# A conditioned mixture-of-experts layer on one core: the first batch's h in plain f32, casts in another place, and the last rows weighed by VectorE and TensorE

## The reference

```python
h = einsum('bsi,bio->bso', x, W[id]) + b[id][:, None, :]      # (4, 256, 256), 16 experts of W, one for each batch
y = swiglu(h, sw1, sw2, sw3)                                   # shared: silu(h @ sw1) * (h @ sw3) @ sw2, width 352
scores = softmax(h @ gate_w)                                   # 8 experts, each row takes its two highest
for e in range(8):
    y = y + cw[:, e:e + 1] * swiglu(h, rw1[e], rw2[e], rw3[e]) # width 176; cw is 0 where e was not chosen
out = x + y
```

## Time and profile before

| | us |
|---|---|
| median of 3 runs (lowest, highest) | 115.42 (114.95, 117.1) |
| the profiled execution: its own time | 114.82 |
| the profiled execution: its span | 113.2 |

### The profile page before, as it was taken

How to read it: one execution, slowest core, us unless ns; L and a number is a source line. 1 busy time by engine, 2 the same in 40 slices (tenths; PEclk the granted TensorE clock), 3 DMA queues, 4 the chain that set the end, 5 groups by cost and what they waited for, 6 DMA issues and landing times.

```text
span 113.2 us, 2194 instructions
## 1 busy us (share of the span) xinstructions
PE 104.1 (92%) x608; PEld 88.2 (78%) x608; DVE 68.0 (60%) x220; ACT 52.2 (46%) x131; POOL 47.7 (42%) x63
## 2 busy tenths in 40 slices
PE   6997998499999978999999999999999999999870
PEld 4776887466688856677889998999999997888650
DVE  1034864546999079878877775684754533123991
ACT  4044673762660295366655753456556545102200
POOL 5280078872777200005653345335535536703610
PEclk9999999959999999999999999999999999999999
DMA  2897999996988446431232424231021120029935
GB/s 36 247 309 240 349 362 360 372 393 174 228 254 274 185 142 188 125 110 60 93 133 73 143 84 136 88 128 54 5 93 40 52 92 0 0 23 381 376 122 210
DMA packets 16736, 19.07 MB, mean 168 GB/s; under 512 B 2338, under 2 KB 13718, under 8 KB 16726
## 3 DMA queue, kind: packets, MB, share of 16 engines
q1 hardware_dynamic: 13302, 12.62, 36.3%
q0 software_dynamic: 1984, 4.46, 11.2%
q10 hardware_dynamic: 1440, 1.86, 4.9%
HBM read 12.64 MB, written 7.21 MB: 175 GB/s over the span
## 4 chain that ended last, share of the span: by engine, by line
PE 60%; ACT 8%; DVE 7%; another core or an unknown queue 7%; issue 6%; DMA 5%; POOL 3%; POOLq 1%; DVEq 0%; ACTq 0%
PE bank L858 42%; PE bank L870 6%; DVE x_area L815 5%; PE bank L1027 4%; PE bank L992 4%; ACT w_all L494 4%; DMA y_area<-_out_by_choice_and_token 3%; ACT cond_area L462 2%; DMA _out_by_choice_and_token<-y_area,dest 2%; ACT hT_area L443 1%; PE bank L885 1%; PE bank L888 1%; POOL _out_by_choice_and_token L412 1%; POOLq L289 1%
## 5 line engine op out<-in xcount | busy, mean ns | idle before, releaser
L412 POOL DMA_INDIRECT _out_by_choice_and_token<-y_area,dest x23 | 23.6, 1025 | 38.0 <-DVE y_area L771 26.3
L858 PE MATMUL bank<-w_all,hsT_hi 128*128 x72 | 21.6, 342 | 0.0
L396 POOL DMA_INDIRECT rows_by_expert<-h_area,slot x16 | 15.7, 978 | 12.8 <-DVE slot L634 8.7
L858 PE MATMUL bank<-hT_area,sh_area 128*128 128x512 f32 (+1 forms) x72 | 18.6, 418 | 0.0
L858 PEld LDWEIGHTS bank<-hT_area,sh_area 128*128 128x128 f32 (+1 forms) x72 | 13.4, 190 | 4.1 <-DVE sh_area L552 0.3
L858 PEld LDWEIGHTS bank<-w_all,hsT_hi 128*128 128x128 f32 x72 | 13.0, 188 | 0.0
L765 DVE TENSOR_TENSOR y_area<-y_area,bank 128x176 f32<-128x176 f32 x23 | 7.7, 336 | 7.3 <-issue 4.2
L509 ACT ACTIVATE y_area<-bank 128x176 f32<-128x176 f32 x23 | 7.3, 317 | 10.2 <-PE bank L858 8.3
L552 DVE TENSOR_TENSOR hsT_lo<-bank,hsT_hi 128x256 fp32r<-128x256 f32 x18 | 7.6, 423 | 6.7 <-ACT hsT_hi L505 5.5
L858 PE MATMUL bank<-w_all,hsT_lo 128*128 x36 | 11.5, 320 | 0.0
L858 PE MATMUL bank<-sh_raw,gated 128*128 128x256 f32 (+1 forms) x48 | 10.8, 380 | 0.6 <-DVE gated L567 0.6
(11 more groups left out here) (130 smaller groups left out, 200.3 us busy)
## 6 DMA issues: line engine op xcount, KB each, us to landing
h_area<-rows_by_expert SPq DMA_DIRECT2D x23, 128.0 KB, 2.0
raw<-in_L_ffn_rw_dram SPq DMA_DIRECT2D x16, 176.0 KB
raw<-in_L_ffn_rw_dram SPq DMA_DIRECT2D x2, 704.0 KB
rows_by_expert<-x_area SPq DMA_DIRECT2D x8, 128.0 KB
y_area<-_out_by_choice_and_token SPq DMA_DIRECT2D x4, 256.0 KB, 4.6
y_area<-_out_by_choice_and_token ACTq DMA_DIRECT2D x4, 256.0 KB, 5.0
out_dram<-x_area SPq DMA_DIRECT2D x3, 256.0 KB, 2.0
sh_raw<-in_L_ffn_sw_dram SPq DMA_DIRECT2D x2, 352.0 KB, 4.2
```

The lines of the kernel that those rows point to most:

```text
L396: nc.gpsimd.indirect_dma_start(out=rows_dram, out_offset=bass.IndirectOffsetOnAxis(ap=slot[:, i, t:t + 1], axis=0), in_=h_sb[:, t, :], in_ ...
L412: nc.gpsimd.indirect_dma_start(out=y_dram, out_offset=bass.IndirectOffsetOnAxis(ap=dest[:, j:j + 1], axis=0), in_=y_sb[j % NBY], in_offset ...
L858: last = nc.tensor.matmul(dst, w, v, start=start and n == 0, stop=stop and n == len(operands) - 1)
```

## The change

**First batch.** h of batch 0 is kept as plain f32 in a new tile `first_h`; ScalarE makes one half, VectorE the other. `first_h_by_token` forms the gate products of its 256 rows alone and first (four f32 products with 16 columns), and then turns the rows with four f32 transposes. One reduction serves both sets of rows. The rounding of this batch (`hT_hi`, `hT_lo`) is done later, in two wide instructions, before ScalarE's and VectorE's work on batch 3. `ranks(0)` stands before `condition(1, 1)` instead of behind it. VectorE copies the first turned x, and ScalarE the second. GpSimd writes the expert numbers before it makes the identity matrix.

**Casts and table.** ScalarE does all eight `w13_hi_of` before the silu of group 3. VectorE does `at_tile` and the remainders of experts 0 and 1 before `shared_gate(3)`. TensorE does `shared_down(0, 0)` and `turn_rows(0)` before `table()`.

**The end.** ScalarE's copies and GpSimd's additions for batches 2 and 3 are gone. Of each of these batches VectorE adds and weighs the first 128 rows, and TensorE weighs the second 128 rows, its diagonal products being accumulated on the shared down products in PSUM, so that one addition to x remains for them. There are four diagonal matrices instead of six.

The diff, cut to what the text speaks of:

```diff
             nc.gpsimd.memset(ident[:, :], 0.0).then_inc(ident_ready, 1)
             pool.dma_start(ids_bc[:, :], ids.to_broadcast([NE, B])).then_inc(ids_in, 16)
+            nc.gpsimd.iota(expert_no[:, :], pattern=[[0, 1]], base=0, channel_multiplier=1).then_inc(expert_no_ready, 1)
...
-            for b in range(BH, B):
-                pool.wait_ge(acc_sb_ready, b - BH + 1)
-                x_row = x_sb[:, b].rearrange("p j d -> p (j d)")
-                nc.gpsimd.tensor_tensor(x_row, acc_sb[b - BH][:, :], x_row, ALU.add).then_inc(late_base_ready, 1)
...
-            xT_of(0)
+            xT_of(1)
...
-            hT_hi_of(0, 0)
-            hT_hi_of(0, 1)
+            act.wait_ge(h_ready, 1)
+            act.wait_ge(biasT_ready, 1)
+            nc.scalar.activation(first_h[:, 0, :], h_ps[0][0], ACT.Identity, bias=biasT[:, 0, 0:1]) \
+                .then_inc(first_h_act, 1)
...
             hT_hi_of(2, 1)
+            act.wait_ge(first_h_dve, 1)
+            nc.scalar.copy(hT_hi[:, :, 0:S], first_h[:, :, :]).then_inc(first_hi_ready, 1)
             hT_hi_of(3, 0)
...
-                if 1 <= g <= E // 2:
-                    w13_hi_of(2 * g - 2)
-                    w13_hi_of(2 * g - 1)
+                if g < 2:
+                    w13_hi_of(2 * g)
+                    w13_hi_of(2 * g + 1)
+                if g == 2:
+                    for e in range(4, E):
+                        w13_hi_of(e)
...
-            for b in range(BH, B):
-                act.wait_ge(acc_ready, JS * (b + 1))
-                nc.scalar.copy(acc_sb[b - BH][:, :], acc_ps[b]).then_inc(acc_sb_ready, 1)
...
-            hT_lo_of(0, 0)
-            hT_lo_of(0, 1)
+            dve.wait_ge(h_ready, 2)
+            dve.wait_ge(biasT_ready, 1)
+            nc.vector.tensor_scalar(first_h[:, 1, :], h_ps[0][1], biasT[:, 1, 0:1], None, ALU.add).then_inc(first_h_dve, 1)
             two_highest_of(0)
...
             hT_lo_of(2, 1)
+            dve.wait_ge(first_hi_ready, 1)
+            lo_part(hT_lo[:, :, 0:S], first_h[:, :, :], hT_hi[:, :, 0:S]).then_inc(first_lo_ready, 1)
             hT_lo_of(3, 0)
...
-            shared_gate(3)
             after("tile")
...
-            shared_gate(4)
             w13_lo_of(0)
             w13_lo_of(1)
+            shared_gate(3)
+            shared_gate(4)
             shared_gate(5)
...
                 for i in range(TOPK):
                     for j in range(JS):
                         weigh(b, i, j)
+                base_of(B - 1 - b, 0, 2 * JS + 1 + b)
...
+                dve.wait_ge(y_in[b], 16 * TOPK)
+                dve.wait_ge(base_ready, JS + 3)
+                for i in range(TOPK):
+                    weigh(b, i, 0)
+                dve.wait_ge(weighed_ready, b - BH + 1)
+                nc.vector.tensor_tensor(x_sb[:, b, 1, :], y_acc[b][1], x_sb[:, b, 1, :], ALU.add).then_inc(out_ready, 1)
...
+            def first_h_by_token():
+                pe.wait_ge(first_h_act, 1)
+                pe.wait_ge(first_h_dve, 1)
+                pe.wait_ge(ident_ready, 3)
+                pe.wait_ge(gate_lo_ready, 1)
+                for t in range(JS):
+                    last = add_products(first_gate_ps[:, 2 * E * t:2 * E * t + 2 * E],
+                                        [(first_h[:, k, t * P:(t + 1) * P],
+                                          turn_and_gate[:, P + k * GW:P + k * GW + 2 * E].bitcast(F32)) for k in range(KD)],
+                                        True, True)
+                last.then_inc(first_gate_ready, 1)
+                for t in range(JS):
+                    for k in range(KD):
+                        last = nc.tensor.transpose(htok_ps[t][:, k * GW:k * GW + P], first_h[:, k, t * P:(t + 1) * P],
+                                                   ident[:, :])
+                    last.then_inc(htok_ready, 1)
...
-            h_by_token(0)
+            first_h_by_token()
             condition(1, 0)
+            ranks(0)
             condition(1, 1)
-            ranks(0)
...
-            table()
             shared_down(0, 0)
             turn_rows(0)
+            table()
...
-            for b in range(1, B):
-                for j in range(JS):
+            for j in range(JS):
+                shared_down(1, j)
+            pe.wait_ge(late_y_ready, NTILE - FIRST_DOWN)
+            for j in range(JS):
+                for b in reversed(range(BH, B)):
                     shared_down(b, j)
```

More of the change, by code:

```diff
@@ L759, in _ @@
             dve.wait_ge(filled, 16 * E)
-            base_of(0, 0)
+            base_of(0, 0, 1)
             dve.wait_ge(weighing, 3)
@@ L802, in _ @@
                     w2_lo_of(s - 2)
-                if E + 4 <= s < E + 4 + NT // 2 and s - E - 4 + NT // 2 != JS * (B - 1):
+                if E + 4 <= s < E + 4 + NT // 2 and (s - E - 4) % JS == 1:
                     diagonals_of(s - E - 4 + NT // 2)
-            base_of(0, 1)
-            dve.wait_ge(acc_ready, JS * BH)
+            base_of(0, 1, 2)
+            dve.wait_ge(acc_ready, 2 * JS)
             x_row = x_sb[:, 1].rearrange("p j d -> p (j d)")
-            nc.vector.tensor_tensor(x_row, acc_ps[1], x_row, ALU.add).then_inc(base_ready, 1)
+            nc.vector.tensor_tensor(x_row, bank[4][:, :], x_row, ALU.add).then_inc(base_ready, 1)
             def weigh(b, i, j):
@@ L903, in shared_up @@
                     pe.wait_ge(gated_ready, g - 2)
+                if g == 0 and w == 0:
+                    pe.wait_ge(first_lo_ready, 1)
                 toks = slice(h * HT, (h + 1) * HT)
```

92 lines of the change are left out of this document (42 added, 50 removed).

## The result

The changed kernel took 114.06 us (median of 20 runs, 113.3 to 117.02), the kernel before in the same hours 114.96 (20 runs): the ratio is 0.9924, 95% interval 0.9900 to 0.9949. That is 0.9 us less, half of the 1.8 us predicted, within 2%. On another chip, later, the same kernel stood at 0.9994 (0.9960 to 1.0029), 114.31 us.

A forecast was written before the change was run, and what follows sets the result against it. TensorE, busy at full clock from 44.70 to 96.60 us, was taken as the bound, with gains only before and behind that. -1.25 + 0 - 0.55 = -1.8 us from the 115.42 median gave 113.6, range 110.9 to 115.8 (8 in 10).

The forecast's parts named there:

- the join: Before the routed tiles: reordered casts, remainders and table bring the first up product from 44.70 to 43.45 us, gaining 1.25.
- The prediction's own signs: Right: first `raw,hsT` product near 43.4 us, no row releaser above 0.3; wrong: dispatches longer than 1.1 us around 37.
- by the row it is 0.46 us for one such meeting, less than the 0.9 us to spare: At the join, the last dispatch beside `at_tile` and remainders may end 0.46 us later; its rows have 0.9 to spare.
- rival (d): At the join, `at_tile` and remainders hold the last dispatch 2.23 us; clock may fall; 116.6 us, slower; chance 0.07.
- The first batch: Start of the kernel, first h and its gate products: 0 us, from -0.6 to +0.6.
- The end: VectorE's weighings and additions for the last rows take 6.6 us against 7.2, a gain of 0.55 us.
- rival (b): At the end, landing transfers make the long weighings, so they stay; 115.8 us, no change; chance 0.08.
- (a): Wait at 19.3 to 21.3 us was chance or moves with order; low clock may go too; 111.6 us; chance 0.20.
- (c): The join gives only half because a shared group's signal comes later than TensorE's end; 114.3 us; chance 0.13.

The follow-up runs named there:

- lo_late_again: The same kernel as `lo_late`, run on another chip beside the changed kernel itself; 113.05 us, ratio 0.9881 to the kernel before.
- lo_late: Changed kernel with the remainders of experts 0 and 1 put back between `shared_gate(4)` and `shared_gate(5)`, `at_tile` staying early; 112.45 us, ratio 0.9974 to the kernel before.
- part_first: Kernel before with only the first batch's part of the change; 112.46 us, ratio 1.0009 to the kernel before.
- store_held: Changed kernel with SyncE's first store of results held until batch 3's gathered results have landed; 114.24 us, ratio 0.9987 to the kernel before.
- part_join: Kernel before with only the casts and table part of the change, VectorE's new order included; 116.04 us, ratio 1.0181 to the kernel before.
- lo_first: Changed kernel with the remainders of experts 0 and 1 ahead of `at_tile` instead of behind it; 114.22 us, 4 runs, no interval.
- lo_early_before: Kernel before with only VectorE's new order: `at_tile` and two remainders ahead of `shared_gate(3)`; 115.38 us, ratio 1.0173 to the kernel before.
- after_again: The changed kernel itself, run again on another chip as yardstick; 114.31 us, ratio 0.9994 to the kernel before.
- part_end: Kernel before with only the end part of the change, for the last rows; 114.21 us, ratio 1.0134 to the kernel before.
- dve_old: Changed kernel with VectorE's order of before at the join (`shared_gate(3)`, `at_tile`, `shared_gate(4)`, two remainders, `shared_gate(5)`); 112.01 us, ratio 0.9928 to the kernel before.
- dve_old_sh_early: As `dve_old`, with `sh_lo_of(1)` also moved from ahead of `shared_gate(0)` to ahead of `slots_of(2)`; 112.33 us, ratio 0.9927 to the kernel before.
- part_end_warm: `part_end` with twelve products of unused results between `shared_down(0, 0)` and `turn_rows(0)`; 115.67 us, ratio 1.0115 to the kernel before.
- the second group: Four runs on one chip: `after_again`, `lo_late_again`, `store_held` and `part_end_warm`, against the kernel before at 114.43 us.

## Why the prediction was right, and where it was not

**The total** came out with the right sign and half the size: 114.06 against 113.6, inside the range and within 2%. The range of 110.9 to 115.8 was wide enough to hold no change at all, and the largest term of the sum, the join, failed, so that the total came out inside it is in part luck. The prediction's own signs say so: the first up product stood at 44.64 and not near 43.4, rows were its releaser for 0.92 us, and a dispatch of over 1.1 us near 37 was named as a sign of being wrong. The terms as the first profile shows them, 0.06 us at the join and 0.2 at the end (0.6 where the rows had landed), do not add up to 0.9 either; where the rest comes from is open.

**The join: the gain of 1.25 us was there and was given back.** By the steps: the gates come two together and then one, `shared_down(0, 0)` starts at 41.16 (predicted 41.01) without a wait. From there to the first up product `lo_late_again` needs 2.34 us; predicted was 43.45 - 41.01 = 2.44. The kernel before needed 44.70 - 41.01 = 3.69, so the edit's own worth is 1.35 us where TensorE comes to the join as late as in these two profiles; with an early TensorE it was nothing (`lo_late` against `part_first`). What failed is the sentence "by the row it is 0.46 us for one such meeting, less than the 0.9 us to spare". There was one dispatch, but it met three instructions in a row, 0.53 + 1.68 us, and was held for all of them: 3.24 - 0.96 = 2.28 us, where rival (d) had 2.23. The row of one meeting gave the price of a meeting with the rest of one remainder, not with a run of instructions. Rival (d) predicted the rows at 43.6 (43.55) and a first up product at 44.7 (44.64). Its second half, the fall of the clock, did not happen in the profiles of the changed kernel and `store_held`, whose wait is 0.90 to 0.99 us; it did in `part_join`, `lo_first` and `lo_early_before`, where TensorE came earlier. I gave this rival 0.07, although the rows carried it and a rule spoke for it: the Trainium skill ("SBUF — State Buffer", section "SBUF: two separate sides") has the two engines lock one another out for a whole instruction, and the trace agrees here, for three such instructions back to back: the dispatch ended 0.84 us after the last. Two things in it are not so plain: the dispatch had begun 0.27 us ahead of `at_tile` and was held all the same, and not every overlap holds one (last section).

**The first batch: 0, as said.** `part_first` gives 1.0009. The steps: the gate products last 1.04 us (1.0), TensorE is through at 10.79 (10.6), the marks stand at 11.95 (11.8), TensorE waits 0.38 us for them (0.3). What stands behind did not stay where it stood: the second batch's `h_by_token` starts at 14.74, 0.6 us later than before; the wait for the last half of h took that up, 1.21 instead of 1.92.

**The end: VectorE's work was as predicted where the rows had landed, but the gain in time is not shown.** VectorE takes 6.61 to 6.62 us in eight profiles (`after_again`, `store_held`, `lo_first`, `lo_late`, `lo_late_again`, `part_end`, `dve_old`, `dve_old_sh_early`), predicted 6.6, against 7.21, 7.22 and 7.82 with the old end. The long weighings went with GpSimd's additions, and the DMA engines are as busy in these us as before (1.00 to 1.05 from 104 to 107 in the changed kernel, 1.03 to 1.06 in the kernel before), so rival (b) falls. In the first profile of the changed kernel and in `part_end_warm` 0.41 and 0.75 us went to waits for landing rows or for TensorE, and 0.2 us was what remained of the 0.6 in the former. As time the term has no run that shows it: on the chip of the second group the changed kernel has the short end and stands at 0.9994, and `part_end_warm` less its products is where the kernel before is.

**Rivals (a) and (c).** The half clock behind 22 us was gone, as (a) has it, but ScalarE's wait was not: the same instruction waits 1.23 us, and 1.57 us of a new wait at 29.91 took the clock's gain. Since the same code up to there shows 0.23 us in the profiles of two other chips (`part_end`, `lo_early_before`), and `part_end_warm`, without the new first batch, has 1.89 and 1.19 us, these waits belong to the execution and the chip and not to the change. Why a signal comes late there stays open. (c) is not needed: the gates were in time.

Still open: why the changed kernel stood at 0.9924 on one chip and 0.9994 on another. Of the dispatch both have the same 3.24 us, and both profiles have a late TensorE. The kernel before has no profile on the second chip, and on the first its executions have no clock on record but the profiled one's (0.985).

## What to carry to other kernels

When work with two SBUF operands is moved into an engine's idle time, look at what GpSimd issues in that time: a dispatch that it meets can be held until the whole run of such instructions is over, and if a chain of dispatches and a load feeds the next stage, what exceeds the chain's slack is paid: here 1.2 us for a dispatch of 3.24 instead of 1.61. A gap on one engine is free only for work that no other engine's chain can feel. And price such a meeting by the run of instructions that the dispatch meets, not by the one row at hand.

## What was not expected

A dispatch is not held by everything that overlaps it. `sh_area`'s remainder of 128x512, also with two SBUF operands, held one when it began 0.12 to 0.23 us ahead of it and left it at 0.96 when it began 0.11 to 0.27 us behind it (eleven profiles); `at_tile` and the 128x704 remainders held it when they began 0.20 to 0.28 us behind it, and `at_tile` at 0.31 did not (`dve_old_sh_early`). A gate product of 128x512, with one operand in PSUM, began 0.21 to 0.26 us behind a dispatch in `part_first`, `part_end` and `dve_old` and left it at 0.96 to 1.01. No run changed the operands of one and the same instruction, so that it is the two SBUF operands that count is argued from these meetings, not tested by itself. In `part_end` the remainder held two dispatches in a row:

```profile
25.54 1.29 POOL L392 DMA_INDIRECT rows_by_expert<-h_area,slot  x1 [0.31 <-issue]
27.14 1.40 POOL L392 DMA_INDIRECT rows_by_expert<-h_area,slot  x1 [0.30 <-issue]
```
```profile
25.31 0.67 DVE L540 TENSOR_TENSOR sh_area<-sh_raw,sh_area 128x512 fp32r<-128x512 f32 x1
27.02 0.68 DVE L540 TENSOR_TENSOR sh_area<-sh_raw,sh_area 128x512 fp32r<-128x512 f32 x1
```

Both end 0.85 and 0.84 us after the remainder. What tells the harmless overlaps from the others is not settled.

The length of one wait does not tell whether the granted clock falls. It fell to 0.50 after 1.91 us in `part_end`, after 0.63 and 1.38 us with the shared products between them in `lo_first`, and stayed at 1.00 after this, in `dve_old`:

```profile
40.70 1.53 PE L868 MATMUL bank<-sh_raw,gated 96*128 96x256 f32 x6 [2.46 <-issue]
42.67 0.44 PE L1017 MATMUL bank<-ident,h_area 128*128 128x128 f32 x2 [0.43 <-DMA h_area<-rows_by_expert]
```

This execution took 114.14 us, 2.1 over its kernel's median. No releaser is named for the 2.46 us, but `shared_down(0, 0)` also waits for the shared down weights (`sh2_in`), and the last of the six gates was done by 39.04. SyncE's load of these weights (time of issue), and its us to landing:

```profile
28.37 1.59 SPq L339 DMA_DIRECT2D sh_raw<-in_L_ffn_sw_dram  x1
sh_raw<-in_L_ffn_sw_dram SPq DMA_DIRECT2D x1, 256.0 KB, 12.2
```

That is 40.57, and TensorE starts at 40.70. In `lo_first` the same load lands at 26.87 + 11.9 = 38.77, and TensorE starts at 38.83 after its 0.63 us. So where TensorE comes early, the load of these weights, which my sum did not have, can hold it as well.
